# Selective scan kernel: the old y is added by TensorE inside the sum over states, and ScalarE copies y out

## The reference

```python
def step(h, inp):
    u_t, d_t, b_t, c_t = inp
    dA = jnp.exp(d_t[..., None] * A)
    h = dA * h + (d_t * u_t)[..., None] * b_t[:, :, None, :]
    y = jnp.einsum('bkdn,bkn->bkd', h, c_t)
    return (h, y)
...
return y + Ds[None, :, :, None] * xs
...
y = out_y[:, 0] + inv_y[:, 0] + wh_y + invwh_y
```

## Time and profile before

| what | value |
|---|---|
| median of 3 runs | 14746.57 us (14745.5 to 14750.3) |
| the profiled execution, own time | 14743.57 us |
| its span | 14741.9 us |
| DVE busy | 12258.6 us, 83% |
| PE busy | 11069.1 us, 75% |
| POOL busy | 9980.4 us, 68% |
| ACT busy | 6853.8 us, 46% |
| mean granted TensorE clock | 0.858 of full |

### The profile page before, as it was taken

How to read it: one execution, slowest core, us unless ns; L and a number is a source line. 1 busy time by engine, 2 the same in 40 slices (tenths; PEclk the granted TensorE clock), 3 DMA queues, 4 the chain that set the end, 5 groups by cost and what they waited for, 6 DMA issues and landing times. The chain is left out here.

```text
span 14741.9 us, 97052 instructions
## 1 busy us (share of the span) xinstructions
PE 11069.1 (75%) x24688; PEld 4294.8 (29%) x24688; DVE 12258.6 (83%) x8679; ACT 6853.8 (46%) x10234; POOL 9980.4 (68%) x4293
## 2 busy tenths in 40 slices
PE   7777877778777787777877778777787777877777
PEld 2222322223222232222322223222232222322222
DVE  6999579995799957999579995799957999579995
ACT  4444444444444444444444444444444444444444
POOL 3898348982489824898248982489824898248982
PEclk8888888888888888888888888888888888888888
DMA  4676336763366633666336663466634666346662
GB/s 127 199 208 200 88 119 200 207 199 84 120 200 207 200 84 120 200 206 201 82 122 201 206 201 80 123 201 206 200 79 125 202 204 203 76 128 201 205 202 73
DMA packets 693750, 2391.49 MB, mean 162 GB/s; under 512 B 137088, under 2 KB 137088, under 8 KB 683264
## 3 DMA queue, kind: packets, MB, share of 16 engines
q1 hardware_dynamic: 693152, 2384.91, 54.2%
HBM read 2300.09 MB, written 67.11 MB: 161 GB/s over the span
## 5 line engine op out<-in xcount | busy, mean ns | idle before, releaser
L1058 POOL TENSOR_TENSOR state<-state,c_sb 128x1024 f32<-128x1024 f32 x3072 | 7190.5, 2356 | 1094.6 <-ACT carry L870 1092.8
L831 PE MATMUL ps<-state,wt 128*128 128x512 f32 x12288 | 6722.7, 689 | 1108.3 <-DVE ya L984 629.4
L831 PEld LDWEIGHTS ps<-state,wt 128*128 128x128 f32 x12288 | 2697.6, 224 | 4186.3 <-issue 2624.9
L1014 DVE TENSOR_TENSOR_SCAN state<-decay,carry,ps 128x1024 f32<-128x1024 f32 x1440 | 3379.3, 2347 | 51.3
L1047 POOL TENSOR_TENSOR dbu<-b_sb,du 128x1024 f32<-128x1024 f32 x1152 | 2710.4, 2353 | 892.9 <-DVE du L1031 892.9
L870 ACT COPY carry<-state 128x1 f32<-128x1 f32 x3072 | 588.4, 192 | 5726.8 <-DVE state L1014 5717.7
L808 PE MATMUL ps<-parts,sel 114*128 114x512 bf16 (+1 forms) x3840 | 1383.7, 448 | 1786.9 <-DVE state L1014 1780.1
L1001 DVE TENSOR_TENSOR ps<-ps,du 128x1024 f32<-128x1024 f32 x1920 | 2327.5, 1212 | 401.8 <-PE ps L808 401.0
L911 ACT ACTIVATE decay<-delta,a_neg 128x1024 f32<-128x1024 f32 x1920 | 2194.9, 1144 | 6.2
L1014 DVE TENSOR_TENSOR_SCAN state<-ps,carry,dbu 128x1024 f32<-128x1024 f32 x864 | 2016.0, 2333 | 2.6 <-ACT carry L870 2.6
L911 ACT ACTIVATE ps<-delta,a_neg 128x1024 f32<-128x1024 f32 x1152 | 1277.9, 1109 | 0.0
(11 more groups left out here) (179 smaller groups left out, 10118.3 us busy)
## 6 DMA issues: line engine op xcount, KB each, us to landing
c_sb<-bc SPq DMA_DIRECT2D x2048, 512.0 KB, 4.0
c_sb<-bc SPq DMA_DIRECT2D x2048, 256.0 KB, 4.6
b_sb<-bc SPq DMA_DIRECT2D x768, 512.0 KB, 4.7
b_sb<-bc SPq DMA_DIRECT2D x768, 256.0 KB, 5.1
x_nat<-x SPq DMA_DIRECT2D x17, 1536.0 KB, 9.0
gates<-gate_a SPq DMA_DIRECT2D x8, 2048.0 KB, 6.4
gate_a<-gates SPq DMA_DIRECT2D x8, 2048.0 KB, 9.1
x_tok<-x SPq DMA_DIRECT2D x288, 48.0 KB, 1.7
```

What stands on the lines that cost most here:

```text
L831: mm = pe.matmul(py[:, q * CH:(q + 1) * CH], col("ident"), state[:, slot(g, n), q * CH:(q + 1) * CH], start=(n == 0), stop=(n == NS - 1))
L1014: dve.tensor_tensor_scan(state[:, slot(g, n), way], rate, what, 0.0 if fresh else carry[:, n:n + 1], ALU.mult, ALU.add)\
L1058: pool.tensor_tensor(state[:, slot(g, n), :], state[:, slot(g, n), :], c_sb[:, n % CRING, :], ALU.mult).then_inc(S["weighted"], 1)
```

## The change

- `take_y` moves from DVE to ACT. There it is one copy from `py` to `ya` or `yr`, in step `Y_AT` = 6, in the place that the Ln of softplus had in the ACT queue.
- What it added is now added by PE: after the last state of a chunk, `add_y` issues two more products of 512 columns into `py`, with the identity and the old y (T = 1, 3, 4, 5) or with a diagonal matrix of D and u (T = 0, 2). For T = 1 and 4 they read `ya` in steps of 64 elements. They raise a new semaphore `y_summed`, for which ACT's copy waits.
- `RING` goes from 6 to 7 and `LAG` from 5 to 6. The seventh slot is that of `log_z`; the Ln now works in place in `zexp`, and so waits for DVE's reading of it (`dt_low`) and moves to step 9.
- `conv_diag` gives up its permanent place. POOL rebuilds it for each image in `prep_a` by nine products of 128x128; two diagonal matrices `d_diag` are built once by DVE.

```diff
-RING = 6
+RING = 7
-LAG = 5
+LAG = 6
-Y_AT = 4
+Y_AT = 6
+LN_AT = 9
...
                 def _(pool):
                     for i in range(2):
                         pool.memset(pad[i][:, :, :], 0.0).then_inc(S["pads_zero"], 1)
+                    for t in range(9):
+                        pool.tensor_tensor(conv_diag[:, t, :], col("ident"), conv_w[:, t:t + 1].broadcast_to([128, 128]),
+                                           ALU.mult)
...
                             mm = pe.matmul(py[:, q * CH:(q + 1) * CH], col("ident"),
                                            state[:, slot(g, n), q * CH:(q + 1) * CH],
-                                           start=(n == 0), stop=(n == NS - 1))
+                                           start=(n == 0), stop=False)
                         mm.then_inc(S["summed"], 1)
+                        if n == NS - 1:
+                            add_y(g // NSC, chunk_at(g // NSC, g % NSC)).then_inc(S["y_summed"], 1)
+
+                    def add_y(T, at):
+
+                        old = (ua, None, ur, ya, None, yr)[T]
+                        for q in range(2):
+                            o = py[:, q * CH:(q + 1) * CH]
+                            if T % 3 == 1:
+                                by_col = ya[:, :].rearrange("p (h w) -> p w h", w=W)[:, rows(2 * at + q), :]
+                                mm = pe.matmul(rc(o), col("ident"), by_col, start=False, stop=True)
+                            else:
+                                mm = pe.matmul(o, d_diag[:, T // 2, :] if T in (0, 2) else col("ident"),
+                                               old[:, sl(2 * at + q)], start=False, stop=True)
+                        return mm
...
+                    def take_y(T, at, g):
+
+                        if g == 0:
+                            act.wait_ge(S["parts_in"], 24 * 16)
+                            act.wait_ge(S["bc_stored"], 12 * 16)
+                        act.wait_ge(S["y_summed"], g + 1)
+                        act.copy(chunk(yr if T % 3 == 2 else ya, T, at), like(py[:, :], T)).then_inc(S["y_taken"], 1)
...
-                        act.activation(log_z[:, :], zexp[:, :], ACT.Ln, bias=col("one")).then_inc(S["dt_ln"], 1)
+                        act.wait_ge(S["dt_low"], g + 1)
+                        act.activation(zexp[:, :], zexp[:, :], ACT.Ln, bias=col("one")).then_inc(S["dt_ln"], 1)
...
                                 carry_on(previous[0], g - 1, NS - 1)
+                            if n == Y_AT and previous:
+                                take_y(previous[0], chunk_at(*previous), g - 1)
...
-                                if n == PRE_AT + 4:
+                                if n == LN_AT:
                                     softplus_ln(g + 1)
...
-                            if n == Y_AT and before:
-                                take_y(*before, g - 1)
```

More of the change, by code:

```diff
@@ L117, in build @@
     wt = put("wt", [128, n_cols], F32)
-    conv_diag = put("conv_diag", [128, 9, 128], F32)
+    conv_w = put("conv_w", [128, 9], F32)
+    d_diag = put("d_diag", [128, 2, 128], F32)
     sel = put("sel", [XR3, NS, 2 * 128], BF16)
@@ L179, in build @@
     gn_small = at("gn_small", [C, 64], F32, C0)
+    conv_diag = at("conv_diag", [128, 9, 128], F32, C0 + 512 + 20480)
     rest = at("rest", [PIECE, SLOTS, CH], F32, C0 + 512)
@@ L201, in scan_buf @@
         return at(name, [128, SC] if ring is None else [128, ring, SC], F32, first)
-    delta, du, relu_v, log_z, zexp = map(scan_buf, ("delta", "du", "relu_v", "log_z", "zexp"))
+    delta, du, relu_v, zexp = map(scan_buf, ("delta", "du", "relu_v", "zexp"))
     decay, state, c_sb, b_sb, dbu = (scan_buf(n, r) for n, r in (("decay", 2), ("state", RING), ("c_sb", CRING),
@@ L251, in build @@
         ps = [[t[:, s * CH:(s + 1) * CH] for s in range(SLOTS)] for t in ps2]
-        names = """w_loaded w_in_loaded post_w_loaded setup_act setup_dve setup_pool
+        names = """w_loaded w_in_loaded post_w_loaded setup_act setup_dve setup_pool setup_d
         x_nat_in x_tok_in gn_stats gn_dve mean_mm gn_mm gn_act scales_ready x_turned gn_scaled gn_ready
@@ L259, in build @@
         pre_mm dt_abs dt_relu dt_exp dt_one dt_ln dt_low dt_high delta_sum delta_ready du_ready
-        b_mm decayed dbu_ready dbu_pooled scanned carried weighted summed y_taken
+        b_mm decayed dbu_ready dbu_pooled scanned carried weighted summed y_summed y_taken
         c_in_0 c_in_1 c_in_2 c_in_3 b_in_0 b_in_1
@@ L301, in _ @@
                 dve.wait_ge(S["w_loaded"], 64 + 16 * GROUPS)
-                for t in range(9):
-                    nc.vector.tensor_scalar(conv_diag[:, t, :], col("ident"), scol(setup, "conv_w")[:, t:t + 1],
-                                            None, ALU.mult)
+                nc.vector.tensor_copy(conv_w[:, :], scol(setup, "conv_w"))
                 for half in range(2):
@@ L318, in _ @@
                 nc.vector.tensor_tensor(dt_w[:, 2, :, :], dt_r[:, :, :], dt_w[:, 1, :, :], ALU.subtract)
-                nc.vector.tensor_reduce(d_sum[:, :], scol(setup, "ds"), AX_X, ALU.add)
+                nc.vector.tensor_reduce(d_sum[:, :], scol(setup, "ds"), AX_X, ALU.add).then_inc(S["setup_d"], 1)
+                dve.wait_ge(S["setup_d"], 1)
+                for i in range(2):
+                    nc.vector.tensor_scalar(d_diag[:, i, :], col("ident"), d_sum[:, i:i + 1], None, ALU.mult)
                 nc.vector.tensor_copy(w1_q[:, :], scol(setup, "w1_t", C), saturate=False)
@@ L863, in _ @@
                     ln_exp_tables(act)
-                    act.sem_inc(S["carried"], CREDIT)
+                    for q in ("carried", "y_taken"):
+                        act.sem_inc(S[q], CREDIT)
+                    def take_y(T, at, g):
[4 more added lines that the diff above has]
+                        act.copy(chunk(yr if T % 3 == 2 else ya, T, at), like(py[:, :], T)).then_inc(S["y_taken"], 1)
                     def carry_on(T, g, n):
@@ L938, in _ @@
                     carry_on(5, 6 * NSC - 1, NS - 1)
+                    take_y(5, 0, 6 * NSC - 1)
                 @block.vector
                 def _(dve):
-                    for q in ("scanned", "y_taken"):
-                        dve.sem_inc(S[q], CREDIT)
+                    dve.sem_inc(S["scanned"], CREDIT)
                     def u_of(T, at):
@@ L962, in softplus_sum @@
                         dve.wait_ge(S["dt_ln"], g + 1)
-                        dve.tensor_tensor(pc[:, :], log_z[:, :], pc[:, :], ALU.add).then_inc(S["delta_sum"], 1)
+                        dve.tensor_tensor(pc[:, :], zexp[:, :], pc[:, :], ALU.add).then_inc(S["delta_sum"], 1)
                     def next_du(T, at, g):
@@ L970, in next_du @@
                            .then_inc(S["du_ready"], 1)
[L972 to L984, removed]
                     def steps(T, c, previous, following):
                         g = c + T * NSC
-                        before = (previous[0], chunk_at(*previous)) if previous else None
                         after = (following[0], chunk_at(*following)) if following else None
@@ L1032, in _ @@
                     each_chunk(steps)
-                    take_y(5, 0, 6 * NSC - 1)
                 @block.gpsimd
```

## The result

| what | before | after |
|---|---|---|
| median | 14748.43 us (14745.5 to 14751.87, 4 runs) | 14416.79 us (14403.9 to 14427.02, 4 runs) |
| ratio to before | | 0.9775, 95% interval 0.9758 to 0.9792 |
| profiled execution, own time | 14743.57 us | 14427.02 us |
| span | 14741.9 us | 14425.4 us |
| mean granted clock | 0.858 | 0.874 |

The account below looks back on a forecast made before the run. DVE was taken to bound the kernel in the scan, with one wait a chunk for PE. The terms gave 14743.6 - 285 - 123 + 12 = 14348 us, so 14350 us as the median; range 14110 to 14500 us.

Parts of the forecast that it names:

- What bounds the kernel: Scan: DVE is fullest, 96% busy, with one wait a chunk for a spread of PE, 401.0 us in all.
- The instruction, 285 us: Scan: `take_y` leaves DVE, removing 309.2 - 9.6 - 15 = 285 us.
- the wait, 123 us: Scan: the multiply's wait at state 6 (401 us) goes, one at state 7 (278 us) comes; 123 us saved.
- The rule against it: PE's clock falls once idle; a spread breaks the idleness, so the clock could stay up before the sum of state 0.
- rival B: PE in the scan: the clock stays up, or falls only behind the sum; 14115 us, chance 0.17.
- Image ends, 12 us: Final y of each image: `add_y` adds 1.72 us, the copy is 0.2 us shorter; 8 x 1.5 = +12 us.
- At nothing: No cost from the decay behind ACT's copy, the Ln in step 9, `conv_diag` on POOL, or POOL's pace.
- C: PE in the scan: sums of states 0 and 1 both low, spread of state 8 late; 14588 us, chance 0.12.
- D: Scan: DVE's time comes back as waits on POOL, half a microsecond a chunk; 14445 us, chance 0.08.
- E: Scan: PE becomes the bound, 58.9 us a chunk at 55% low clock; slower, 15220 us, chance 0.05.

Follow-up runs that it names:

- e1: Changed kernel with ACT's copy of y one step earlier (step 5), a softplus step moved behind the carry of state 5; 14098.8 us.
- e2: Changed kernel with PE writing the spread of state 6 four times instead of once; 14205.1 us.
- e6: Changed kernel with ACT writing y plainly in the tiles by columns, so output is out of order there; 14296.4 us.
- e3: Changed kernel with ring and lag back to 6 and 5, y still added by PE and copied by ACT; 15152.1 us.
- e5: Changed kernel without the two products of `add_y`, so the output lacks these terms; 14432.9 us.
- e4: Changed kernel with y taken by DVE in step 4 again, add included; ring 7, lag 6 and the Ln in step 9 stay; 14341.0 us.
- e7: Changed kernel with ACT's copy in step 4, ring and lag back to 6 and 5, softplus steps one later; 14262.6 us.

## Why the prediction was right, and what it mis-sized

**What bounds the kernel** held: DVE in the scan, with one wait a chunk. In e1, where that wait is gone, the plain chunks in the middle of a tile take 53.03 us. The spacings of the earlier trace rows give 53.2 for DVE's instructions alone: ten scans with a multiply at 3.48, six pooled scans at 2.26, and four more instructions, softplus and `du`, at 1.2.

**The instruction, 285 us, and the wait, 123 us.** From the first scan to the last, the first image took 228.16 to 1582.10 before and 231.91 to 1540.44 after, 45.4 us less; over the eight images it is 366 us, where the two terms come to 408. The 42 us between lie in the second term, that of the waits: the waits at the scan are 317 us instead of 278. What is left for the first, the instruction, is 288 us against the 285 forecast (366 less the 78 by which the waits of the multiply and of these scans fell together, from 404 to 326). The step that was mis-sized is "with a high part in some chunks: 1.2 us a wait for plain chunks, 2.1 for those that take y by columns". In the first image the plain chunks wait 1.4 us on average and most of them exactly 1.67, the column chunks 2.4. The low stretch covered the whole sum in most chunks: in 135 of 184 all four records of the sum are spaced as at the low level, in 41 some are, in 8 none. At the low level throughout, the prediction's own bound was 352 us. The mechanism, the line, the releaser and the longest wait (2.8 against 2.5 forecast) were as stated.

**The rule against it.** By the Trainium skill (TensorE: Matmul & The Clock Gate, section on the HAM clock gate) the clock falls when the engine has stood idle, so that the spread between the two idle stretches might have kept it up. That was rival B, 14115 us. This kernel's rows decide against it: the sum behind 1.25 and 2.77 us of idleness, with 0.6 us of work between them, ran at the low level. e2 shows that more work at that very place keeps it up, and e6 that with 2.48 us of idleness behind the spread it goes either way. What decides there stays open.

**Image ends, 12 us.** It was 30: the time from the last scan to the first DVE instruction of the next block grew from 15.5 to 20.5 us in the first image (start to start, 1582.10 to 1597.63 and 1540.44 to 1560.92), and by 3.8 us on average over the eight. This term was too small, too. PE there, and DVE:

```profile
1534.83 1.04 PE L815 MATMUL ps<-parts,sel 114*128 114x512 bf16 x2 [2.97 <-DVE state L1033]
1535.66 16.50 PE L838 MATMUL ps<-state,wt 128*128 128x512 f32 x32
1552.00 1.88 PE L854 MATMUL ps<-yr,wt 128*128 128x512 f32 x4
```

```profile
1540.44 2.33 DVE L1033 TENSOR_TENSOR_SCAN state<-ps,carry,dbu 128x1024 f32<-128x1024 f32 x1
1560.92 0.69 DVE L1242 TENSOR_TENSOR ya<-ya,ps 128x512 f32<-128x512 f32 x1 [18.16 <-PE ps L1112]
```

The term counted `add_y` alone, and for that it was right: in e3, with the short lag, each end is 1.5 us longer than before. With a lag of six PE comes to the last spread with eight sums to do, after 2.97 us of idleness, and does them in 16.5 us, the first of them low; before, it was through at the pace of POOL. In e1, with the clock up, POOL sets the pace again, and this end costs 2.8 us less than here, the eight on average 1.6. So of the 3.8 us, 1.5 are `add_y`, 0.7 the longer lag and 1.6 the clock.

**At nothing.** The nine products on POOL take 0.40 us each, and POOL still sits idle for 454 us in 8 waits after them:

```profile
L606 POOL MEMSET parts<- 96x4096 bf16 x16 | 60.0, 3781 | 453.8 <-POOLq L416 453.8
...
L429 POOL TENSOR_TENSOR conv_diag<-wt,conv_w 128x128 f32<-128x128 f32 x72 | 26.1, 400 | 0.3
```

The column-wise copy was taken at 1.95 us and is 1.92. `add_y` in the scan: no delay in the rows of the plain chunk; e5 agrees but can't price it by itself. The Ln in step 9 makes no wait of DVE.

**The rest.** Of the 79 us by which the profiled execution (14427.0) missed the 14348 of the sum, 42 are the scan's wait and 18 the image ends. The other 19 lie outside the scans, in blocks which the change doesn't touch but for the POOL products; no run was made on them, and their cause stays open. That execution was the slowest of four, 10 us above their median.

**The rivals.** B failed on the clock. C (the spread of state 8 late as well) didn't come: 7.8 us of waits for spreads. D (POOL sets the pace) didn't: no wait for POOL, even in e1 at 53 us a chunk only 4.2 us. E didn't: PE's mean clock rose from 0.858 to 0.874, and DVE still waits for one sum a chunk only.

## What to carry to other kernels

When work leaves the engine that is the bound, write down when its result is ready in its new place and who stands behind that; here the new queue position was worth more (318 us, e1) than the freed instruction (285 us). A wait of a few microseconds on PE can cost twice, once as itself and once in the clock of what follows, so look first for what could release it earlier on the releasing engine's own queue. Test the parts of a change apart, and each at more than one place: the lag alone (e4) beat the whole; the move alone was slower than doing nothing with the copy in step 6 (e3), and faster than lag and whole with the copy in step 4 (e7).

## What was not expected of the hardware

- Waits that depend on PE's clock come out equal over many chunks: in the first image nine waits at the scan are 1.66 or 1.67 us, and seven chunks last 54.80 or 54.81 us. In each of these nine the granted clock is low from at least 1.4 us before the end of the copy to at least 4.7 us after it, while the sum is done 3.83 us after it: the whole sum is low, and the wait is at its ceiling. Where the fall comes moves by 0.7 us between them without moving the wait. The prediction had taken an average over where the fall may come, and that gave too small a wait.
- Useless work made the kernel faster: six more products a chunk (e2) took 212 us off.
- After the same spread and the same 2.48 us of idleness, the same eight products took 6.57 us in one chunk and 3.70 in the next (e6).
- Leaving useful work out made nothing faster (e5), and the mean granted clock fell from 0.874 to 0.851.
